# Row moments of the first spline stage made as the second zone stage ends its rows

## The reference

```python
def _layernorm(x, axis=-1, eps=1e-05):
    m = jnp.mean(x, axis=axis, keepdims=True)
    v = jnp.var(x, axis=axis, keepdims=True)
    return (x - m) / jnp.sqrt(v + eps)
...
x = x + 0.5 * _L0_ffn_ref(_layernorm(x), ...)     # zones_a
x = x + _L0_attn_ref(_layernorm(x), ...)          # splat
x = x + 0.5 * _L0_ffn_ref(_layernorm(x), ...)     # zones_b
x = x + 0.5 * _L1_ffn_ref(_layernorm(x), ...)     # spline_a
x = x + _L1_attn_ref(_layernorm(x), ...)          # causal
x = x + 0.5 * _L1_ffn_ref(_layernorm(x), ...)     # spline_b
```

## Time and profile before

| | before |
|---|---|
| median of three runs | 1563.82 us |
| the profiled execution's own time | 1563.83 us |
| its span, first to last instruction | 1562.0 us |
| PE busy | 1433.0 us (92%) |
| DVE busy | 1202.8 us (77%) |
| ACT busy | 986.4 us (63%) |
| POOL busy | 465.3 us (30%) |
| first and last split (L922) of the second zone stage begin at | 964.9 and 1225.3 us |
| first and last bend of ACT in the first spline stage begin at | 1243.2 and 1329.6 us |

### The profile page before, as it was taken

How to read it: one execution, slowest core, us unless ns; L and a number is a source line. 1 busy time by engine, 2 the same in 40 slices (tenths; PEclk the granted TensorE clock), 3 DMA queues, 4 the chain that set the end, 5 groups by cost and what they waited for, 6 DMA issues and landing times. The chain is left out here.

```text
span 1562.0 us, 43828 instructions
## 1 busy us (share of the span) xinstructions
PE 1433.0 (92%) x14442; PEld 1040.8 (67%) x14443; DVE 1202.8 (77%) x2634; ACT 986.4 (63%) x1478; POOL 465.3 (30%) x694
## 2 busy tenths in 40 slices
PE   1699999978999999999999987999999799799697
PEld 1499999955666666666666655999999544699443
DVE  8688888847778887877887854888888697587695
ACT  5366566534666666666666654665665399577597
POOL 6321221211222222222222202211221298222585
PEclk9999999988999999999999998999999899899899
DMA  5000000000000000000000000000000000000011
GB/s 237 1 1 0 0 0 0 0 1 1 2 2 2 1 0 0 0 0 0 0 0 1 2 2 2 1 0 0 0 0 0 1 0 1 1 0 1 8 47 54
DMA packets 9527, 14.40 MB, mean 9 GB/s; under 512 B 368, under 2 KB 8560, under 8 KB 8688
## 3 DMA queue, kind: packets, MB, share of 16 engines
q1 hardware_dynamic: 9456, 13.44, 2.3%
HBM read 9.25 MB, written 4.19 MB: 9 GB/s over the span
## 5 line engine op out<-in xcount | busy, mean ns | idle before, releaser
L1312 DVE TENSOR_REDUCE neg_max<-splat_fill_ps 128x2 f16<-128x512 f32 x512 | 334.0, 691 | 91.0 <-PE splat_fill_ps L1091 87.0
L1237 ACT ACTIVATE splat_probs<-splat_ring 128x1024 f32<-128x1024 f32 x256 | 248.1, 1021 | 98.3 <-PE splat_ring L1118 98.3
L876 ACT ACTIVATE zones_b_hidden<-zones_b_hidden_ps,gelu_scale 128x1024 f32<-128x1024 f32 x96 | 107.1, 1115 | 85.5 <-PE zones_b_hidden_ps L806 84.2
L876 ACT ACTIVATE zones_a_hidden<-zones_a_hidden_ps,gelu_scale 128x1024 f32<-128x1024 f32 x96 | 107.1, 1115 | 84.8 <-PE zones_a_hidden_ps L806 83.5
L1118 PE MATMUL splat_ring<-splat_queries,splat_keys 32*128 32x256 f32 x2048 | 153.0, 393 | 4.2 <-ACT splat_probs L1237 3.2
L1091 PE MATMUL splat_fill_ps<-splat_keys,splat_queries 32*128 32x256 bf16 x1024 | 146.0, 278 | 6.2 <-DVE neg_max L1312 3.3
L1132 PE MATMUL splat_mixed_ps<-splat_probs,values 128*32 128x256 f32 x2048 | 137.0, 385 | 0.4 <-ACT splat_probs L1237 0.4
L925 DVE SCALAR_TENSOR_TENSOR zones_b_hid_lo<-zones_b_hidden,unit_scale,zones_b_hid_hi 128x1024 f16<-128x1024 f32 x96 | 123.6, 1288 | 3.4
L925 DVE SCALAR_TENSOR_TENSOR zones_a_hid_lo<-zones_a_hidden,unit_scale,zones_a_hid_hi 128x1024 f16<-128x1024 f32 x96 | 123.6, 1288 | 3.4
L133 POOL TENSOR_TENSOR splat_ended_shifted<-splat_ended_moments,eps 128x2 f32<-128x2 f32 x32 | 6.3, 197 | 344.4 <-DVE splat_ended_moments L127 344.4
L1118 PEld LDWEIGHTS splat_ring<-splat_queries,splat_keys 32*128 32x128 f32 x2048 | 100.0, 185 | 11.6 <-ACT splat_probs L1237 4.4
(11 more groups left out here) (356 smaller groups left out, 3498.3 us busy)
## 6 DMA issues: line engine op xcount, KB each, us to landing
x_res<-rows SPq DMA_DIRECT2D x4, 1024.0 KB, 18.8
out<-x_res SPq DMA_DIRECT2D x16, 256.0 KB, 2.3
stage_a<-wa SPq DMA_DIRECT2D x1, 2048.0 KB, 8.8
stage_b<-wb SPq DMA_DIRECT2D x1, 2048.0 KB, 13.2
packed<-table SPq DMA_DIRECT2D x1, 840.0 KB, 4.4
```

Source lines behind the costliest of these rows:

```text
L876: nc.scalar.activation(hidden[k][:, :, :], hidden_ps[of][:, :, :], ACT.Gelu_apprx_tanh, scale=s.gelu_scale[:, :]).then_inc(gelu_done, 1)
L1237: nc.scalar.activation(probs[u % PROB_BUFFERS][:, :, :, :].rearrange("p h k i -> p (h k) i"), ring[u % 2][:, :, :], ACT.Exp).then_inc(exp_ ...
L1312: nc.vector.tensor_reduce(s.neg_max[:, tile, t:t + 2, GROUP * g + SPLATS], fill_ps[f % 2][:, :, :], AX.X, ALU.max, negate=True).then_inc(m ...
```

## The change

In the second zone stage only (`moments=True`), DVE makes the moments of each sample right behind its `add`: `end` waits for its own sum and for a free buffer, then two `bn_stats` and two `bn_aggr`. POOL, behind its `take_half` of a sample four later, makes the reciprocal deviation and copies both columns to `s.mean` and `s.rstd`. In the first spline stage (`normed_before=True`), `statistics` and `power` are gone, `apply` reads `s.mean` and `s.rstd`, and the copy `keep_normed` is a DVE instruction between `keep_inner` and `apply` in place of ACT's. In both zone stages DVE's loop begins two samples later (13 passes in place of 14), and POOL's four later.

```diff
--- before.py
+++ after.py
@@ -732,10 +732,12 @@
                                                         ALU.mult, ALU.add))
                 nc.vector.tensor_copy(s.zone_code[:, :], code[:, :])
 
-def zones(nc, s, stage):
+def zones(nc, s, stage, moments=False):
+
 
     with ExitStack() as ctx:
         sb, ps, sem = sb_maker(nc, ctx), ps_maker(nc, ctx), sem_maker(nc, ctx, stage)
+        ended = RowNorm(nc, s, ctx, stage + "_ended", 0)
         normed = [sb(f"{stage}_normed{i}", [P, TILES, P], F32) for i in range(2)]
         half = sb(stage + "_half", [P, TILES, P], F32)
         norm_hi = [sb(f"{stage}_norm_hi{i}", [P, TOKENS], F16) for i in range(2)]
@@ -769,11 +771,30 @@
                     settle(pool, half_ready, b + 1)
                     nc.gpsimd.tensor_tensor(rows, rows, half[:, :, :], ALU.add).then_inc(x_ready, 1)
 
-                take_half(0, 0)
-                take_half(1, 1)
-                with pairs(pool, 2, SAMPLES) as i:
+                def keep_moments(b, parity):
+                    ended.power(pool, b, parity)
+                    columns = slice(TILES * b, TILES * (b + 1)) if isinstance(b, int) else bass.ds(b * TILES, TILES)
+                    settle(pool, ended.rstd_ready, b + 1)
+                    nc.gpsimd.tensor_copy(s.mean[:, columns], ended.moments[parity][:, :, 0])
+                    nc.gpsimd.tensor_copy(s.rstd[:, columns], ended.rstd[parity][:, :]).then_inc(ended.ready, 1)
+
+
+                for b in range(4):
+                    take_half(b, b % 2)
+                take_half(4, 0)
+                if moments:
+                    keep_moments(0, 0)
+                take_half(5, 1)
+                if moments:
+                    keep_moments(1, 1)
+                with pairs(pool, 6, SAMPLES) as i:
                     for parity in range(2):
                         take_half(i + parity, parity)
+                        if moments:
+                            keep_moments(i + parity - 4, parity)
+                if moments:
+                    for b in range(SAMPLES - 4, SAMPLES):
+                        keep_moments(b, b % 2)
 
             @block.tensor
             def _(pe):
@@ -940,17 +961,28 @@
                         keep_low(b + 2, parity)
                     if not is_first:
                         add(b - 1, 1 - parity)
+                        if moments:
+                            end(b - 1, 1 - parity)
+
+                def end(b, parity):
+                    settle(dve, added, b + 1)
+                    settle(dve, ended.ready, b - 1)
+                    ended.statistics(dve, b, parity)
 
                 keep_low(0, 0)
                 keep_low(1, 1)
                 sample(0, 0, is_first=True)
-                with pairs(dve, 1, LOOP_END) as i:
+                sample(1, 1)
+                sample(2, 0)
+                with pairs(dve, 3, LOOP_END) as i:
                     sample(i, 1)
                     sample(i + 1, 0)
                 sample(SAMPLES - 3, 1)
                 sample(SAMPLES - 2, 0, turns=False)
                 sample(SAMPLES - 1, 1, turns=False)
                 add(SAMPLES - 1, 1)
+                if moments:
+                    end(SAMPLES - 1, 1)
 
 
 def splat_attention(nc, s, stage):
@@ -1414,7 +1446,8 @@
 
 
 
-def splines(nc, s, stage, out=None):
+def splines(nc, s, stage, out=None, normed_before=False):
+
 
 
     PAIRS = SAMPLES // 2
@@ -1463,7 +1496,20 @@
 
                 def apply(p, parity):
                     wait(dve, turned_ready, p - 1)
-                    norm.apply(dve, p, parity, normed[parity])
+                    if normed_before:
+                        for t in range(PAIR):
+                            column = bass.ds(p * PAIR + t, 1)
+                            last = nc.vector.tensor_scalar(normed[parity][:, t, :], pair_of(s.x_res, p, t),
+                                                           s.mean[:, column], s.rstd[:, column],
+                                                           ALU.subtract, ALU.mult)
+                        last.then_inc(norm_ready, 1)
+                    else:
+                        norm.apply(dve, p, parity, normed[parity])
+
+                def keep_normed(p, parity):
+                    dve.wait_ge(turned_ready, p + 1)
+                    wait(dve, inner_a_ready, p - 1)
+                    nc.vector.tensor_copy(normed_t[parity][:, :], turned[:, :]).then_inc(normt_ready, 1)
 
                 def keep_inner(p, parity):
                     dve.wait_ge(inner_b_ready, p + 1)
@@ -1485,7 +1531,10 @@
                     nc.vector.tensor_tensor(rows, rows, result[parity][:, :].rearrange("p (t d) -> p t d", t=PAIR),
                                             ALU.add).then_inc(added, 1)
 
-                run(dve, (keep_inner, 1), (apply, 3), (statistics, 4), (add, -1))
+                if normed_before:
+                    run(dve, (keep_inner, 1), (keep_normed, 2), (apply, 3), (add, -1))
+                else:
+                    run(dve, (keep_inner, 1), (apply, 3), (statistics, 4), (add, -1))
                 add(PAIRS - 1, 1)
 
             @block.gpsimd
@@ -1507,7 +1556,10 @@
                     rows = pair_of(s.x_res, p)
                     nc.gpsimd.tensor_tensor(rows, rows, s.half_bias[:, :, :], ALU.add).then_inc(biased, 1)
 
-                run(pool, (bend, 1), (power, 4), (bias, 2))
+                if normed_before:
+                    run(pool, (bend, 1), (bias, 2))
+                else:
+                    run(pool, (bend, 1), (power, 4), (bias, 2))
 
             @block.tensor
             def _(pe):
@@ -1582,7 +1634,10 @@
                     act.wait_ge(inner_b_kept, p + 1)
                     bend_some(p, parity, ((0, 2), (0, 3), (1, 0), (1, 2))).then_inc(bent_act, 1)
 
-                run(act, (bend_first, 0), (keep_summed, -1), (bend_rest, 0), (keep_normed, 2))
+                if normed_before:
+                    run(act, (bend_first, 0), (keep_summed, -1), (bend_rest, 0))
+                else:
+                    run(act, (bend_first, 0), (keep_summed, -1), (bend_rest, 0), (keep_normed, 2))
                 keep_summed(PAIRS - 1, 1)
 
             if out is not None:
@@ -1832,9 +1887,9 @@
         recycle(nc)
         splat_attention(nc, s, "splat")
         route(nc, s, "route_b")
-        zones(nc, s, "zones_b")
+        zones(nc, s, "zones_b", moments=True)
         recycle(nc)
-        splines(nc, s, "spline_a")
+        splines(nc, s, "spline_a", normed_before=True)
         causal_attention(nc, s, "causal")
         splines(nc, s, "spline_b", out)
```

## The result

| | before | after |
|---|---|---|
| median | 1562.95 us (1561.74 to 1566.64, 5 runs) | 1574.32 us (1571.79 to 1574.53, 5 runs) |
| profiled execution, its span | 1563.83, 1562.0 us | 1572.16, 1570.4 us |
| PE, DVE, ACT, POOL busy | 1433.0, 1202.8, 986.4, 465.3 us | 1438.7, 1198.8, 977.5, 560.1 us |

After over before is 1.0064, with a 95% interval of 1.0048 to 1.0080: slower, by some 10 us. The profiled pair differs by 8.4 us in the span, and the medians by 11.4; what follows is reckoned within the profiled pair.

A forecast was written before the change was run, and what follows sets the result against it. TensorE was taken to bound the second zone stage, a TensorE-ScalarE cycle the spline stage. From 1563.83 us: 6.2 (loop branch) + 0.2 (last sample) + 2.3 (stage end) - 3.8 (spline start) + 0 = 4.9, so 1568.7 us; range 1560 to 1575.

The forecast's parts named there:

- collision: Rival, chance 0.10: GpSimd's new instructions and VectorE's splits get in each other's way, about 9 us more, 1577.7 us.
- TensorE as the bound, and the chain through the sum: Second zone stage: TensorE never waits; VectorE's sum waits for TensorE's turned result, so VectorE's lateness recurs in each sample.
- In the middle seam ... Cost nothing; the cover is that room: Sample change inside the loop body: split 0.86 to 0.93 us late against 1.05 of room, so no cost.
- The room: How late VectorE's split may be before TensorE loses time: 1.05 us mid-body, 0.57 us over the loop's branch.
- hand-over of 0.14: Time from a late split's end to TensorE's next product, 0.14 us, read at the end of the zone stage.
- Across the branch: Sample change over the loop's branch: split at 1.87 to 1.94 us, TensorE waits 0.50 each, 12.5 times, 6.2 us.
- End of the stage: After the zone stage's last sum, VectorE's block (0.94) and GpSimd's part (1.35) add 2.3 us.
- last sample: VectorE some 0.9 us late at the zone stage's last sample, mostly absorbed in its waits for ScalarE: 0.2 us lost.
- Start of the spline stage: Statistics gone ahead of the first normalisings: first knot sum 3.3 us sooner, second 0.5 more, 3.8 us gained.
- The ring: Spline stage: TensorE's knot sum and ScalarE's kept sum and bends set turns of 5.48 us; taking ScalarE's copy gains nothing.
- The hidden branch: Rival, chance 0.27: VectorE's sequencer passes the loop's branch while aggregations wait, so the 6.2 us go: 1562.5 us.
- ScalarE as the bound: Rival, chance 0.10: ScalarE bounds the spline stage, so its shorter list gains 6.2 us: 1562.5 us.

The follow-up runs named there:

- the dose: The kernel after, with the block's two batch statistics issued twice per ended sample, the repeats into a buffer nobody reads: 1585.09 us, ratio 1.014.
- the written-out list: The kernel after, with VectorE's second zone stage written out for all samples, so no loop branch and waits on constants: 1563.9 us, ratio 1.0009.
- the spline half alone: The kernel before with only the first spline stage changed (stored columns, VectorE copies the turned rows), no moments made in the zone stage: 1560.08 us, ratio 0.9978.

## Why the prediction was right, and where it was short

The time lies in the range of 1560 to 1575, but 5.6 us above the forecast and above the forecast's own 1566 to 1572. It is slower by over 0.3%, to which I gave 0.40, less than the 0.50 for no measurable change. That it still lies in the range is in part luck: the range reached up to 1575 for the sake of a collision that didn't happen, and what filled it is a cost that the forecast had put at nothing. By its own list of signs the prediction was wrong at one point: "Wrong if ... every sample has one", and every sample of the loop has a gap on TensorE.

- **TensorE as the bound, and the chain through the sum**: right, and shown by the dose: each 0.38 that VectorE is late comes back in full.
- **"In the middle seam ... Cost nothing; the cover is that room"**: the step that failed. It costs 0.34 in each of 13 seams, 4.4 us. The block's price was read in the splat stage (0.75) and its waits from places where no register is set just ahead of the waiting instruction (0.03 to 0.10). Here the written-out list and the run without GpSimd's part show 0.26 more ahead of the statistics, 0.20 of it for the register and the wait that stand behind the wait for the sum, and 0.19 more behind the aggregations: before, these last steps ran beside the sum, and now only the short aggregations stand in front of them. The split starts at 1.65, not at 1.20 to 1.27. My bound for it, 0.1 in 13 samples, was under a third of that.
- **The room**: 1.05 and 0.57 were too large. Loss against split start is one line in three kernels (1.44, 1.65, 2.03 against 0.14, 0.34, 0.72), and it meets zero at 1.31 in the middle; across the branch 1.72 and 2.10 against 0.48 and 0.86, zero at 1.24. That is 0.97 and 0.41 of room. The hand-over of 0.14 was one of the stage's end; in the loop of the kernel after, 0.20 passes between the split's end (1086.65 + 1.28) and the product (1088.13), and behind the branch seam 0.30 (the second half from 1095.33, so 1096.61, to 1096.91). With these hand-overs the rooms of the earlier trace rows are 0.99 and 0.41. Why the second is longer isn't shown.
- **Across the branch**: 0.48 against my 0.50, but by two errors that cancel. The split starts at 1.72, not 1.87 to 1.94: branch and registers together add 0.51 to the 1.21 of the written-out list, 0.06 ahead of the statistics and the rest behind the aggregations. And the room is 0.16 smaller.
- **End of the stage** (2.37 against 2.3) and **last sample** (0.1 against 0.2): right.
- **Start of the spline stage**: 3.4 against 3.8. The 2.93 between two normalisings is what TensorE's turnings show, 2.92 (1246.04, 1248.96). The gain depends on when TensorE's clock rises: the first knot sum came 1.44 us later in the spline half alone, where it rose later.
- **The ring**: right. The copy's move changes only how long ScalarE waits.
- **The rivals.** The hidden branch fell: 0.51 of it is seen. ScalarE as the bound fell (the spline half alone). The collision fell for VectorE: its splits keep 0.75 and 1.28 with GpSimd's power beside them. The opposite happened, as below. The Trainium skill (Advanced Engine Details and Errata, Control Flow Timing) gives a compare-and-branch about 0.11 us; added to the written-out list by itself, the seam would have cost nothing. No run shows the branch by itself. The seam with it is 0.28 longer behind the aggregations than the one in the body (0.63 against 0.35), with the loop's own register instructions in it, so the figure can't stand for the whole end of a pass.

What stays open is the 3 us between the 8.4 of the profiled pair and the 11.4 of the medians. The last knot sum is 1.3 of it if most executions of before took 1.92 there, as the ten profiles of the experiments did; that isn't shown.

## What to carry to other kernels

Where the bound engine runs without a gap, look for the place where the helper already waits, and put new work ahead of that wait and not behind it: the same four instructions cost 10 us in the one place and nothing in the other. In a loop, look at what the sequencer does between two instructions (registers set, waits, the branch) and whether a long instruction still runs beside it; here that was 0.45 us in the middle seam and 0.51 across the branch, against a room of 0.97 and 0.41 for block and steps together. Written out, the block behind the sum cost nothing either. And where an engine waits in every turn of a ring, a copy taken from it gives nothing; look instead at who is waited for while the pipeline fills.

## What the hardware showed beside that

GpSimd's small instructions stretch while VectorE splits, and VectorE's splits don't. By line, from 980 to 1213 us (count, busy us, mean ns), in the kernel after:

```profile
L137 POOL TENSOR_TENSOR zones_b_ended_rstd<-zones_b_ended_shifted,minus_half 128x2 f32<-128x2 f32 x27 | 36.4, 1348 | 3.2 <-POOL zones_b_ended_shifted L133 2.1
L778 POOL COPY mean<-zones_b_ended_moments 128x2 f32 (+1 forms) x27 | 29.4, 1089 | 5.9 <-POOL zones_b_ended_rstd L137 5.8
L946 DVE SCALAR_TENSOR_TENSOR zones_b_hid_lo<-zones_b_hidden,unit_scale,zones_b_hid_hi 128x1024 f16<-128x1024 f32 x81 | 104.0, 1284 | 2.9
```

At the end of the stage, with VectorE idle, the same power and the same copy take 0.70 and 0.18:

```profile
1242.58 0.70 POOL L137 TENSOR_TENSOR zones_b_ended_rstd<-zones_b_ended_shifted,minus_half 128x2 f32<-128x2 f32 x1
1243.34 0.18 POOL L778 COPY mean<-zones_b_ended_moments 128x2 f32<-128x2 f32 x1
```

Two columns of 128 rows cost GpSimd 1.35 and 1.09 us in the mean beside a float16 split, while the split's second half keeps its 1284 ns. So GpSimd's busy time over the kernel rose by 94.8 us for work that takes 1.35 us a sample by itself, 43 us in all. GpSimd had the time: it was busy in 45.26 of 233 us before. The Trainium skill (SBUF — State Buffer, Who interferes with whom) says that VectorE in a two-port mode and GpSimd block each other wholly, whoever is second. Which mode a split runs in, no trace here shows. For these small instructions the trace agrees in one direction: who pays is GpSimd. It agrees in the other as well where GpSimd works longer: in the spline stage of the kernel before, VectorE's bend at 1274.39, begun 0.06 after GpSimd's bias (1274.33, for 1.27), took 1.49 and not 0.55 us. In the kernel after all 16 bends take 545 to 548 ns.
